# Decoder layer: scores in four row tiles of TensorE, keys cut 128+128+52, half of the heads' softmax from ScalarE

## The reference

```python
Q = (query @ Wq.T).reshape(B, T_q, N_HEADS, D_HEAD)      # 16 heads of 32
K = (context @ Wk.T).reshape(B, T_c, N_HEADS, D_HEAD)    # T_c = 77
V = (context @ Wv.T).reshape(B, T_c, N_HEADS, D_HEAD)
scores = jnp.einsum('bqhd,bkhd->bhqk', Q, K) / sqrt(D_HEAD)
attn = jax.nn.softmax(scores, axis=-1)
out = jnp.einsum('bhqk,bkhd->bqhd', attn, V).reshape(B, T_q, D)
return out @ Wo.T
```

## Time and profile before

| what | value |
|---|---|
| median of three runs | 2475.74 us (2470.34 to 2476.79) |
| the profiled execution's own time | 2468.48 us |
| its span, first to last instruction | 2466.4 us |
| mean granted TensorE clock | 0.986 |
| TensorE busy (matmuls) | 2373.7 us, 96% of the span |
| VectorE / ScalarE / GpSimd busy | 47% / 38% / 19% |

### The profile page before, as it was taken

The page is one execution under the profiler, slowest core; times in us unless marked ns, Lnnn a source line. Parts: engine busy times, 40 slices in busy tenths (PEclk is TensorE's granted clock), DMA queues, the critical chain, the costliest instruction groups (busy, mean ns, idle before and its releaser), DMA issues.

```text
span 2466.4 us, 32984 instructions
## 1 busy us (share of the span) xinstructions
PE 2373.7 (96%) x11592; PEld 1960.9 (80%) x11592; DVE 1171.2 (47%) x1977; ACT 943.5 (38%) x1504; POOL 466.5 (19%) x554
## 2 busy tenths in 40 slices
PE   8778799999999999999999999999999999999999
PEld 4777578888888887788888888888888888888887
DVE  5999688888888887532222212222222212212211
ACT  3997445444444443433223222223222222323321
POOL 3787222222222222111001001101101101101100
PEclk9988899999999999999999999999999999999999
DMA  9554601101111112400000000000010010000000
GB/s 344 173 186 174 217 1 69 44 34 68 44 53 49 39 52 69 162 1 35 34 15 19 34 19 15 34 34 0 34 34 0 34 34 0 34 34 0 34 17 17
DMA packets 83116, 141.23 MB, mean 57 GB/s; under 512 B 18023, under 2 KB 18535, under 8 KB 82663
## 3 DMA queue, kind: packets, MB, share of 16 engines
q1 hardware_dynamic: 83072, 140.68, 16.4%
HBM read 79.42 MB, written 61.24 MB: 57 GB/s over the span
## 4 chain that ended last, share of the span: by engine, by line
PE 89%; DVE 4%; ACT 3%; POOL 2%; issue 2%; DMA 1%; ACTq 0%; POOLq 0%; SPq 0%; DVEq 0%
PE ps L360 77%; PE ps L1503 5%; PE ps L1483 2%; POOL xu L639 1%; PE ps L1397 1%; ACT tu L770 1%; ACT tu L771 1%; PE ps L1333 1%; PE ps L1416 1%; PE ps L1359 1%; POOL yd L633 0%; DVE ql L1018 0%; DVE xt L1018 0%; DVE es L1196 0%; DVE rmax L1194 0%
## 5 line engine op out<-in xcount | busy, mean ns | idle before, releaser
L1018 DVE TENSOR_TENSOR gtl<-ps,gth 128x512 fp32r<-128x512 f32 x256 | 177.1, 692 | 1089.1 <-ACT gth L907 1089.1
L360 PE MATMUL ps<-xt,wuh 128*128 (+1 forms) x2048 | 638.5, 393 | 5.0 <-DVE xt L1018 4.9
L905 ACT ACTIVATE ps<-ps,up_b 128x512 f32<-128x512 f32 x256 | 169.5, 662 | 990.5 <-PE ps L360 990.5
L360 PEld LDWEIGHTS ps<-xt,wuh 128*128 128x128 f32 x2048 | 383.6, 188 | 93.5 <-DVE xt L1018 8.9
L360 PE MATMUL ps<-wdl,gth 128*128 128x512 f32 x1024 | 402.2, 393 | 0.0
L360 PE MATMUL ps<-wdh,gtl 128*128 128x512 f32 x1024 | 402.1, 393 | 0.0
L360 PE MATMUL ps<-wdh,gth 128*128 128x512 f32 x1024 | 402.0, 393 | 0.0
L360 PE MATMUL ps<-xt,wul 128*128 (+1 forms) x1024 | 400.7, 391 | 0.0
L608 POOL TENSOR_TENSOR rstd<-var_e,mhalf 128x4 f32<-128x4 f32 x48 | 53.2, 1109 | 1300.3 <-DVE var_e L1007 1300.3
L669 POOL TENSOR_TENSOR es<-es,rinv 128x308 f32<-128x308 f32 x256 | 170.9, 699 | 446.3 <-DVE rinv L1207 446.3
L360 PEld LDWEIGHTS ps<-wdh,gth 128*128 128x128 f32 x1024 | 192.2, 188 | 44.1
(11 more groups left out here) (186 smaller groups left out, 3753.5 us busy)
## 6 DMA issues: line engine op xcount, KB each, us to landing
x<-x_scratch SPq DMA_DIRECT2D x32, 1024.0 KB, 5.6
xa<-in_x SPq DMA_DIRECT2D x16, 1024.0 KB, 5.4
x_scratch<-xa SPq DMA_DIRECT2D x16, 1024.0 KB, 4.3
x_scratch<-x SPq DMA_DIRECT2D x16, 1024.0 KB, 4.3
out_x<-x SPq DMA_DIRECT2D x16, 1024.0 KB, 4.3
xu<-in_wexpT SPq DMA_DIRECT2D x4, 1024.0 KB, 18.5
yd<-in_wcon SPq DMA_DIRECT2D x4, 1024.0 KB, 9.9
wd_scratch<-fold SPq DMA_DIRECT2D x4, 1024.0 KB, 6.9
```

The source lines that it names most:

```text
L360: mm = pe.matmul(bank, a, b, start=first and i == 0, stop=last and i == n - 1)
L905: A(bank, bank, ACT.Gelu, bias=up_b[:, m:m + 1]).then_inc(act_gelu, 1)
L1018: sub = lambda o, a, b: V.tensor_tensor(o, a, b.bitcast(F32), ALU.subtract)
```

## The change

Scores: k is no longer block-diagonal. It is stored with 77 keys (padded to 78, `LP`) for all 128 feature rows, loaded by one DMA per part in place of four, and each head's 32 rows are multiplied by themselves: for each chunk and each of the three products there are four matmuls, one per head, with 32 rows, 78 columns, and a bank of PSUM per head (4 x 78 = 312 columns). That makes 48 matmuls for a tile in place of 12.

Keys: the 308 keys are cut 128+128+52. The third piece goes to one tile `pt2` with its high part in partitions 0 to 51 and its low part from 64 on, against v copied to both places, so that one matmul covers both: 8 matmuls in `values` in place of 9. GpSimd clears `pt2` first.

Softmax: 1/sqrt(32) is folded into Wq. For heads 2 and 3 of each chunk (`HB = 2`) VectorE only finds the negated maxima (`top_ready`), and ScalarE takes exponent, shift and sum in one instruction per head and chunk, straight from PSUM (8 per tile, `exp_ps`). Heads 0 and 1 go as before, with half of the numbers. `scores` then also waits for `exp_ps` of the tile before. The attention's loop is written out for all rounds.

```diff
     KC = D // P
     HPC = P // HD
     CK = HPC * L
-    KP = (CK + 2) // 3
-    CKP = 3 * KP
-    NJ = KC * 3
-    V_AT = [0, 2 * HD, 5 * HD, 9 * HD]
+    LP = L + L % 2
+    KT = CK - 2 * P
+    KB = P // 2
+    KU = KB + 2
+    CKP = 2 * P + KU
+    VW = [2 * HD, HPC * HD, HPC * HD]
+    V_AT = [0, VW[0], VW[0] + VW[1], sum(VW)]
+    assert 2 * L <= P + L and 2 * P < CK <= 2 * P + KB
     MC = HID // P
     LOS = 7
     HIS = 4
...
-    kh = r2.put("kh", [P, 2, KC, CK], F32R)
-    kl = r2.put("kl", [P, 2, KC, CK], F32R)
+    kh = r2.put("kh", [P, 2, KC, LP], F32R)
+    kl = r2.put("kl", [P, 2, KC, LP], F32R)
+    r2.at += 4 * 4 * KC * (CK - LP)
-    vh = r2.put("vh", [KP, KC, V_AT[3]], F32R)
-    vl = r2.put("vl", [KP, KC, V_AT[3]], F32R)
+    vh = r2.put("vh", [P, KC, V_AT[3]], F32R)
+    vl = r2.put("vl", [P, KC, V_AT[3]], F32R)
-    pth = r2.put("pth", [KP, NJ, GT], F32R)
-    ptl = r2.put("ptl", [KP, NJ, GT], F32R)
+    pth = r2.put("pth", [P, 2 * KC, GT], F32R)
+    ptl = r2.put("ptl", [P, 2 * KC, GT], F32R)
+    pt2 = r2.put("pt2", [P, KC, GT], F32R)
...
         def attn_loop(eng, body):
             inside = lambda g: lambda d: 0 <= g + d < NG
-            for g in (0, 1):
-                body(g, inside(g))
-            with eng.Fori(2, NG - 2) as g:
-                body(g, lambda d: True)
-            for g in range(NG - 2, NG + 2):
+            for g in range(NG + 2):
                 body(g, inside(g))
...
         for h in range(HPC):
             r = 0
             while r < L:
-                c, at = divmod(h * L + r, KP)
-                n = min(L - r, KP - at)
-                pieces.append((h, r, n, c, at))
+                c, at = divmod(h * L + r, P)
+                n = min(L - r, P - at)
+                pieces += [(h, r, n, c, at)] + [(h, r, n, c, at + KB)] * (c == 2)
                 r += n
-        assert [(h, c) for h, _, _, c, _ in pieces] == [(0, 0), (1, 0), (1, 1), (2, 1), (2, 2), (3, 2)]
+        assert [(h, c) for h, _, _, c, _ in pieces] == [(0, 0), (1, 0), (1, 1), (2, 1), (3, 1), (3, 2), (3, 2)]
         def split3(pe, bank, parts, first=True, last=True):
...
             def load_k(b):
                 for hl, t in ((0, kh), (1, kl)):
-                    for h in range(HPC):
-                        sp.dma_start(raw(t[h * HD:(h + 1) * HD, b % 2, :, h * L:(h + 1) * L]),
-                                     kt_d[hl, h * HD:(h + 1) * HD, :, b * L:(b + 1) * L]).then_inc(k_loaded, 16)
+                    sp.dma_start(raw(t[:, b % 2, :, 0:L]), kt_d[hl, :, :, b * L:(b + 1) * L]).then_inc(k_loaded, 16)
             def load_v(b):
                 for hl, t in ((0, vh), (1, vl)):
...
                 nc.gpsimd.memset(kh[:, b].bitcast(F32), 0.0)
                 nc.gpsimd.memset(kl[:, b].bitcast(F32), 0.0).then_inc(k_zero, 1)
             pool.wait_ge(v_zero, 1)
+            for j in (2, 3):
+                pool.wait_ge(fold_stored[j], 16 * 2)
+            nc.gpsimd.memset(pt2[:, :, :].bitcast(F32), 0.0).then_inc(p_zero, 1)
             def norm(g, has):
                 if not has(0):
...
                 act.wait_ge(pre_pe, c + 1)
                 A(xt2h[:, c, :], ps[:, 4 + c, :], ACT.Copy).then_inc(pre_hi, 1)
             act.wait_ge(wq_loaded, 16)
-            A(wqh[:, :, :], wq_raw[:, :, :], ACT.Copy).then_inc(wq_hi, 1)
+            A(wqh[:, :, :], wq_raw[:, :, :], ACT.Copy, scale=SCALE).then_inc(wq_hi, 1)
             for n in range(MC, 2 * MC, 2):
                 fold_piece(n)
             for c in range(KC):
...
                 def exp(t):
                     if has(0):
+                        act.wait_ge(top_ready, T * g + t + 1)
+                        for h in range(HB, HPC):
+                            for f in range(KC):
+                                at, j = h * KC + f, f * HPC + h
+                                e = A(es[t % 2][:, f, h * L:(h + 1) * L], ps[:, h, f * LP:f * LP + L], ACT.Exp,
+                                      bias=rmax[:, t % 2, at:at + 1], accum_out=rsum[:, t % 2, j:j + 1])
+                        e.then_inc(exp_ps, 1)
                         act.wait_ge(e_ready, T * g + t + 1)
-                        e = es[t % 2][:, :, 0:CK]
-                        A(e, e, ACT.Exp, scale=SCALE).then_inc(exp_done, 1)
+                        e = es[t % 2][:, :, 0:HB * L]
+                        A(e, e, ACT.Exp).then_inc(exp_done, 1)
                 hi_p(2, -1)
                 hi_p(3, -1)
...
                     if not has(0):
                         return
                     n = T * g + t
-                    sc = ps[:, 0:KC, 0:CK].rearrange("p f (h k) -> p f h k", k=L)
-                    mx = rmax[:, t % 2, :].rearrange("p (f h) -> p f h", f=KC)
+                    sc = ps[:, 0:HPC, 0:KC * LP].rearrange("p h (f k) -> p h f k", k=LP)[:, :, :, 0:L]
+                    mx = rmax[:, t % 2, :].rearrange("p (h f) -> p h f", f=KC)
                     dve.wait_ge(s_done, n + 1)
-                    V.tensor_reduce(mx, sc, AX.X, ALU.max).then_inc(max_step, 1)
+                    V.tensor_reduce(mx[:, HB:], sc[:, HB:], AX.X, ALU.max, negate=True).then_inc(top_ready, 1)
+                    V.tensor_reduce(mx[:, 0:HB], sc[:, 0:HB], AX.X, ALU.max).then_inc(max_step, 1)
                     dve.wait_ge(max_step, n + 1)
-                    V.tensor_tensor(es[t % 2][:, :, 0:CK].rearrange("p f (h k) -> p f h k", k=L), sc,
-                                    mx.unsqueeze(3).broadcast_to([P, KC, HPC, L]), ALU.subtract).then_inc(e_ready, 1)
+                    V.tensor_tensor(es[t % 2][:, :, 0:HB * L].rearrange("p f (h k) -> p h f k", k=L), sc[:, 0:HB],
+                                    mx[:, 0:HB].unsqueeze(3).broadcast_to([P, HB, KC, L]), ALU.subtract).then_inc(e_ready, 1)
                 def sums(t):
                     if not has(0):
                         return
                     n = T * g + t
                     dve.wait_ge(exp_done, n + 1)
-                    V.tensor_reduce(rsum[:, t % 2, :].rearrange("p (f h) -> p f h", f=KC),
-                                    es[t % 2][:, :, 0:CK].rearrange("p f (h k) -> p f h k", k=L), AX.X, ALU.add).then_inc(sum_step, 1)
+                    V.tensor_reduce(rsum[:, t % 2, :].rearrange("p (f h) -> p f h", f=KC)[:, :, 0:HB],
+                                    es[t % 2][:, :, 0:HB * L].rearrange("p f (h k) -> p f h k", k=L), AX.X, ALU.add).then_inc(sum_step, 1)
                     dve.wait_ge(sum_step, n + 1)
+                    dve.wait_ge(exp_ps, n + 1)
                     V.reciprocal(rinv[:, t % 2, :], rsum[:, t % 2, :]).then_inc(rinv_ready, 1)
                 lo_p(2, -1)
...
                             pe.wait_ge(pre_lo, 2 * KC)
                         else:
                             pe.wait_ge(dve_slot, SLOTS * g)
-                        pe.wait_ge(k_loaded, (g // GB + 1) * 16 * 2 * HPC)
+                        pe.wait_ge(k_loaded, (g // GB + 1) * 32)
                     after(pe, e_ready, T * g + t)
+                    after(pe, exp_ps, T * g + t)
                     tok = slice(t * P, (t + 1) * P)
                     b = (g // GB) % 2
                     for f in range(KC):
-                        mm = split3(pe, ps[:, f, 0:CK], [(qh[:, f, tok], ql[:, f, tok], kh[:, b, f, :], kl[:, b, f, :])])
+                        cols = slice(f * LP, (f + 1) * LP)
+                        for i, (q, k) in enumerate(((qh, kh), (qh, kl), (ql, kh))):
+                            for h in range(HPC):
+                                at = slice(h * HD, (h + 1) * HD)
+                                mm = pe.matmul(ps[:, h, cols], q[at, f, tok], k[at, b, f, :], start=(i == 0), stop=(i == 2))
                     mm.then_inc(s_done, 1)
                 def turn_p(t, d):
...
                     for q in range(3):
                         b = bank(P_SLOT[t] + q)
                         for j in range(4):
-                            f, c = divmod(4 * q + j, 3)
-                            mm = pe.transpose(b[0:KP, j * P:(j + 1) * P], es[t % 2][:, f, c * KP:(c + 1) * KP], ident[:, :])
+                            keys = es[t % 2][:, j, q * P:min(q * P + P, CKP)]
+                            mm = pe.transpose(b[0:keys.shape[1], j * P:(j + 1) * P], keys, ident[:, :])
                         slots.done(mm, P_SLOT[t] + q)
                 def turn_x(c):
...
                         pe.wait_ge(dve_slot, SLOTS * g + P_SLOT[3] + 3)
                         pe.wait_ge(v_loaded, (g + GB - 1) // GB * 16 * 2 * len(pieces))
                     b = bank(V_SLOT[f])
-                    passes = [(c, v, pt) for c in (2, 1, 0) for v, pt in ((vh, pth), (vh, ptl), (vl, pth))]
+                    passes = [(c, v, pt[:, KC * c + f, :]) for c in (1, 0) for v, pt in ((vh, pth), (vh, ptl), (vl, pth))]
+                    passes[3:3] = [(2, v, pt2[:, f, :]) for v in (vh, vl)]
                     passes.append(passes.pop(1))
                     for i, (c, v, pt) in enumerate(passes):
```

(27 more changed lines are left out.)

## The result

The changed kernel takes 2477.9 us (median of 15 runs, 2476.28 to 2480.54). The kernel before, run beside it, takes 2473.52 (15 runs, 2469.66 to 2476.79). The ratio is 1.002, with a 95% interval of 1.0012 to 1.0028: 4.4 us slower, inside what I called "within 0.3%". The forecast was 2488, 12.3 us slower. The profiled execution took 2476.39 us, its span is 2474.6. Against the profiled execution of the kernel before, whose span is 2466.4, that is 8.2 us more and not 4.4: that execution took 2468.48 us, 5 us less than the median of its kernel.

A forecast was written before the change was run, and what follows sets the result against it. TensorE was taken to set the pace, with instruction issue bounding the new scores: 16 x (0.45 - 0.92) + 15 x 1.08 + 3.6 = +12.3 us on 2475.7, giving 2488 us. The forecast's own range was 2468 to 2503.

The forecast's parts named there:

- within 0.3%: Whole kernel: outcome within 0.3% of the kernel before, chance 0.16, nearly all where a pair costs 0.050 to 0.055 us.
- 31 x 0.058: Scores tile: 17 of 48 pairs are queued, the other 31 issue at 0.058 us each, 1.80 us.
- +1.08 of scores(1): scores(1), queued late behind the wait for exponents: 2.77 us in place of 1.69, +1.08 a group in 15 groups.
- the faster rival: Scores: issue is not the bound, the array's 1.32 + 0.10 us a tile decides; about 2450 us, chance 0.22.
- Serial loads: Scores: row tiles' loads follow each other, 5.38 us a tile, +222 us, 2698 in all; chance 0.17.
- Changing the tiling: Scores: the change of tiling and back adds 0.10 us a tile.
- Values: Values on TensorE: 8 matmuls in place of 9 for four chunks gain 0.92 us a group.
- Exponents: ScalarE: 0.24 us each (0.13 to 0.44), eight done at 640.8, just when TensorE wants scores(1) at 640.85.
- The rival with ScalarE as the bound: ScalarE: exponents at 0.44 us each make scores(1) wait, +37 us on top, 2525; chance 0.10.
- What the change takes off VectorE is worth nothing by itself: Attention group: TensorE sets the pace, so taking half of shift and sum off VectorE gains nothing by itself.
- The start: Ahead of group 0: clearing `pt2` delays rsqrt, apply2(1) and scores(0), to 282.2 against 278.37; +3.6 us (1 to 7).
- the forecast's lower part: Lower part of the forecast's 2468 to 2503 us, where a pair costs 0.050 to 0.055 us.

The follow-up runs named there:

- run 4: The changed kernel, but each of the 48 pairs of a scores tile loads and computes only 64 of 128 tokens: 2442.55 us.
- run 11: The changed kernel, but each of the 48 pairs of a scores tile loads and computes only 32 of 128 tokens: 2426.97 us.
- run 10: The changed kernel without row tiles and without ScalarE's exponents out of the banks, `pt2` cleared behind rsqrt: 2471.49 us, ratio to before 0.999.
- run 12: The kernel before with scores in row tiles, k laid out for them, loop written out; keys 3 x 103, all heads on VectorE: 2470.86 us, ratio 0.9988.
- Run 5: run 1 with only one head of four getting its exponents out of the banks (`HB = 3`): 2458.15 us, ratio to before 0.9943.
- run 6: run 1 with three heads of four getting their exponents out of the banks (`HB = 1`): 2516.62 us, ratio to before 1.0177.
- run 9: The changed kernel with all four heads on VectorE (`HB = 4`) and `pt2` cleared behind rsqrt: 2466.61 us, ratio to before 0.9976.
- run 1: The changed kernel with GpSimd's clearing of `pt2` moved behind the rsqrt for group 1: 2469.71 us, ratio to before 0.9989.
- run 8: The kernel before with its attention loop written out for all 18 rounds, nothing else: 2474.2 us, ratio 1.0004.
- run 7: The changed kernel with the loops of scores turned, a head's three matmuls one after the other: 2477.22 us, ratio to before 1.0021.

## Why the prediction was wrong

*The step that failed* is "31 x 0.058": that instructions reach TensorE no faster than one pair in 0.058 us once its queue is used up. In the changed kernel 48 pairs take 1.47 us, 0.031 each with everything, and the load paces them: 0.112, 0.058 and 0.04 us for four pairs with 128, 64 and 32 columns (runs 4 and 11). In run 11 all 48 pairs are through in 0.59 us, so issue costs at most 0.012 us a pair, also for scores(1), behind whose wait little can have been queued. I had taken the price from one instance, the distance of two loads behind a wait, and never asked whether that distance was the issue or something of the load itself. The same trace, a little later, has the third load of that stretch 0.11 us behind the second (43.98), the pace of the earlier trace rows:

```profile
44.09 0.36 PEld L1342 LDWEIGHTS ps<-ident,xn 128*128 128x128 f32 x3
```

So the 0.058 was the single distance behind an empty queue, and no train of pairs had shown it. In the changed kernel the first four loads behind such a wait all start within 0.04 us (651.47).

For the same reason the +1.08 of scores(1) did not come: it is queued late, as I said, and takes 1.47 all the same. The Trainium skill ("TensorE: Matmul & The Clock Gate", Measured speedup vs the span model) gives about 4 ns of issue for each tile of a packed group. The traces agree: four matmuls together last 0.29 us where one lasts 0.278. That would have made the faster rival the likeliest.

*What the array does.* The row tiles do load at once. Serial loads (2698) were wrong, and the rival's 1.42 a tile was near: 1.32 for the loads, and 1.47 measured.

*Changing the tiling* was sized at 0.10 a tile; it is about 0.2. In one group, against before: turn_p(0) and (1) ahead of scores +0.17 each, turn_p(3) and project(2) +0.06 and +0.09, project(3) some 0.10, turn_x(2) +0.06, query +0.10. The sum is 0.75 us for four tiles. So scores gain 1.07 (6.95 to 5.88) and 0.75 of it goes back: 0.3 a group remains, as runs 10 and 12 show (0.38 and 0.25).

*Values* gained 0.85 a group (8.52 to 7.67) where I had 0.92: right. *Transposes* at zero: right but for the 0.17 above.

*Exponents.* I had 0.24 us each and "just in time"; they take 0.30, inside my bounds of 0.13 and 0.44. Eight end at 651.2, and scores(1) comes 0.59 us late, 9 us in 15 groups. Run 5 takes four away and the wait is gone; run 6 adds four and it grows by 1.2. The rival with ScalarE as the bound, which I put 37 us higher, is what run 6 makes of it.

*VectorE.* "What the change takes off VectorE is worth nothing by itself" was wrong. It was true of the kernel before. Once values are shorter, VectorE with all four heads is late for the bank of values(2) by 0.44 us a group (run 9), and run 10 shows the same with full-width scores, 0.51. That eats half of what the keys give. Moving one head of four away is enough to get it back: 8.5 us between runs 9 and 5. Two heads get it back as well, but pay 0.59 for it at scores(1).

*The start.* The chain was right, with its size off. I had +3.6 (1 to 7), and scores(0) at 282.2. The clearing began at 279.18, 7.8 us after the issue of the two stores had ended (271.40), where I had counted 5.1 and an issue 2 us earlier. From there the steps are those I gave, up to 287.06. Of the 13.5 us by group 2, 8.7 are there by scores(0) of group 0; run 1 gives 6.1 of the 13.5 back. The other 4.8 are lost in groups 0 and 1, which I had priced like all others: they take 94.8 us, against 90.0 before. The lower clock is there (0.61 in 287 to 330 us against 0.84), but the idle 7.71 us are not its main cause. Run 1, whose TensorE waits 1.41 us in that place, shows 0.66 and loses 4.4 us in the two groups; run 12, with row tiles alone, loses 4.0. Run 10, without row tiles, loses 1.0 (each against the 90.0 before). So most of it comes with the row tiles; why the clock is lower with them there, no run settles. Some 2 us of the 8.7 lie ahead of the first instruction that the change touches: rsqrt for the folding starts at 247.32 in place of 245.19. There the clock in 235 to 240 us is 0.64, against 0.93 before and 0.85 in run 8. Why the dip of the clock falls there was not settled; it is not the written-out loop.

*The sum as measured.* It can only be made between the two profiled spans, 8.2 us apart. The start, with groups 0 and 1: +13.5. In each of the 14 groups from group 2 on: scores and their neighbours 0.75 - 1.07 = -0.32, the wait at scores(1) +0.59, values -0.85; together -0.58, and -8.1 in all, where the traces show -9.1. The feed-forward part: +3.9. That makes +9.3 against 8.2. Set against the terms of the forecast: it had +23.4 for scores (with scores(1)), where 16 x -0.32 = -5.1 came, 28.5 too dear; -14.7 for values, where 16 x -0.85 = -13.6 came; 0 for the wait and +3.6 for the start, where 8.9 and 13.5 came, 18.8 too cheap; and nothing for the feed-forward part, where 3.9 came. (These terms count groups 0 and 1 in two places, so they do not add up to 8.2.) So the time came out near the forecast's lower part by luck, without its mechanism: one large error was mostly cancelled by three others. The mechanism was that of the faster rival, whose 2450 lacked most of the wait, the changes of tiling, 10 us of the start and the feed-forward part.

## What to carry to other kernels

Take a price per instruction from a long run of that instruction, not from the distance of two; if the trace has none, keep it as a bound. When a step moves between engines, size its latency against the wait that it will end (here 0.30 us an exponent on the way to a bank), and move only as much as fits: against none, one head of four gained 8.5 us, two lost 3, three lost 50. And look at what stands in the queue behind a preparatory instruction: a clearing of 1.8 us in front of an rsqrt, with the wait for two stores that it brought, cost 7 to 8 us.

## What the runs showed of the hardware

- Four row tiles of 32 rows load and multiply at the same time. The pace of four pairs follows the columns of the load: 0.112 us for 128, 0.058 for 64, 0.04 for 32, each with a matmul of 78 columns (runs 4 and 11).
- Matmuls of different row tiles leave the order of the program (run 7), and the tile takes 1.49 us in place of 1.47. The Trainium skill ("TensorE: Matmul & The Clock Gate", Part 3: Packing small matmuls, on row and column tiling) says that matmuls start and end in program order without exception; with pairs of one row tile standing together, this trace shows otherwise, and the measurement decides. So a semaphore on the last matmul of such a sequence should not be taken to cover the other tiles without a look.
- Going from whole-array work to row tiles costs 0.09 to 0.17 us, and going back 0.06 to 0.10 (the changed kernel against the one before, group at 645.21).
- ScalarE's exponent with a collected sum is two instructions, of 0.338 and 0.220 us in the mean, one pair every 0.30 us for 77 columns.
- A change that leaves a stage alone in the program can still change its time: 0.27% of the feed-forward part, 3.9 us, in all eleven kernels with the new tiles in SBUF. The cause is open.
